# Router logits with the router's columns as weights, and 19 instead of 18 chunks of the shared network ahead of the expert tiles

## The chip, the cores and the metric

The kernel runs on one core of a Trainium2 chip. The metric is the device time of one execution in microseconds (us). TensorE does the matmuls, VectorE (DVE), ScalarE (ACT) and GpSimd (POOL) the elementwise work, SyncE (SP) starts most DMA transfers. Each engine executes its own list of instructions in program order and waits on semaphores that the other engines raise.

## The reference

```python
h = tok(x)                       # sin/cos of x at 6 frequencies, then a product with W: (4, 512, 192)
h = concat([cls_tok, h])         # 513 positions in each of 4 images
h = h + attn(layernorm(h))       # gated linear attention, elu features, running sums over positions
h = h + ffn(layernorm(h))

# ffn: 8 experts, 2 for each position, and a shared network of width 768
probs = softmax(x @ router_w)
gates, idx = top_k(probs, 2);  gates = gates / sum(gates)
routed = sum over the 2 experts of gate * ((silu(x @ w_gate[e]) * (x @ w_up[e])) @ w_down[e])
shared = silu(x @ ws_gate) * (x @ ws_up) @ ws_down
alpha  = sigmoid(x @ sg_w + sg_b)
return alpha * shared + (1 - alpha) * routed
```

## The kernel before

The positions go through in blocks: block 0 is the class token, blocks 1 to 4 are the four images of 512 positions. Every engine's list is written out by hand in one order.

The first two thirds are the token product. For every image `b` there are 9 groups `k`. POOL rounds (`rounds`, L406), DVE takes the remainder (`remainders`, L768 and L772), ACT takes the sines (`sines`, L477 and L480) and TensorE multiplies (`project(b, k)`, L1308: 24 matmuls, which show as 48 records because an fp32 matmul makes two passes). The features have 3 slots. Between the groups of image `b` each engine does one step of the attention of block `b` and of the router of block `b-1`: `attn1` (transposes of the normed input, L1319 and L1321), `attn2`, `attn2b`, `ranks`, `attn3` (L1364, which needs the keys that ACT's DMA moves, L533), `attn5` and so on to `attn8`. The router of a block is on TensorE `router(a)`, L1435 to L1439: for each of the 4 groups of 128 positions 5 fp32r matmuls, in which the positions are the 128 columns of weights and the 10 router columns stream. DVE's `router` copies the logits (L926), picks the top 2 and forms `dz`; ACT's `router` takes the exponential (L570); DVE's `gates`, `places` and POOL's `scatter` (L436) write every position's row into its expert's slots in DRAM.

After the last projection come the chunks of the shared network, `q` = 0 to 23, six for each image. `up(q)` is two products of 5 fp32r matmuls with 512 columns (L1463 to L1467), ACT takes the silu (L584), DVE multiplies (`hidden`, L1033), `down(q)` is 4 fp32 matmuls (L1501, 8 records). `finish(f)` on DVE (L1041) adds the six chunks of image `f` into H and frees the banks for `down` of the next image. `NQB` = 18 chunks stand ahead of the expert tiles; the attention and the router of block 4 lie between them at the places `Q_X1`, ..., `Q_LG` = 11 (router), `Q_RK` = 12 (ranks). SP then waits for all scatters and loads the slots (`xs`, L361). There are 39 tiles of 128 slots (`tile_x`, L1513 and L1514, `tile_up`, L1531 to L1535, `tile_hidden_t`, L1543, `tile_down`, L1553 and L1555); `down(NQB-2)` and `down(NQB-1)` stand inside the first two. Behind the tiles come the class token's shared network and the other 6 chunks, while the tiles' results return from DRAM (`yin`); DVE's `combine(b)` (L1109 and L1111) adds them, L1280 adds the last image's down product, and SP stores.

Of the kernel before, what the change touches and what calls it, by code (L numbers as in the profile page):

```python
# [16 lines left out]
B = 4  # L17
# [19 lines left out]
NQB = 18  # L37
# [26 lines left out]
XT, GU, HT, YB = (5, 6), (1, 0), 7, 2  # L64
# [17 lines left out]
def build(nc, xT, wT, freqs, cls_tok, packed, wsa, wsb, wds, wea, web, wdea, wdeb, blank, slots, ydram, out):  # L82
    with ExitStack() as ctx:
# [40 lines left out]
        wra_hi, wra_lo, wrb = (sb(n, [P, NR], F32R) for n in ("wra_hi", "wra_lo", "wrb"))  # L124
# [27 lines left out]
        with ExitStack() as fourth:  # L152
# [47 lines left out]
            lg_psum top_step dz_ready ez_ready gt_step oh_ready gates_ready rank_psum rk_ready pos_step slots_ready emap_ready  # L200
# [13 lines left out]
         lg_psum, top_step, dz_ready, ez_ready, gt_step, oh_ready, gates_ready, rank_psum, rk_ready, pos_step, slots_ready, emap_ready,  # L214
# [250 lines left out]
        def _(act):  # L465
# [181 lines left out]
            sines(0, 8)  # L647
            sines(1, 0)
# [3 lines left out]
            for b in range(1, B):  # L652
# [4 lines left out]
                if b >= 2:  # L657
                    router(b - 1)
                sines(b, 3)
# [20 lines left out]

            for q in range(NQB):
# [20 lines left out]
                if q == Q_LG:  # L702
                    router(B)
# [21 lines left out]
        def _(dve):  # L725
# [183 lines left out]
            def router(a):  # L909
# [12 lines left out]
                def wide(t):  # L922
# [3 lines left out]
                next_(dve.tensor_copy(lg[0:TP, 0:nt, :], ps[0:TP, logit_bank(a), 0:16 * nt].rearrange(  # L926
                    "p (t n) -> p t n", n=16)[:, :, 0:NE + 1]))
# [330 lines left out]
            finish(2)  # L1258
# [29 lines left out]
        def _(pe):  # L1288
            def project(a, k):
# [8 lines left out]
                for i in range(6):  # L1298
# [13 lines left out]
                ins.then_inc(tok_group, 1)  # L1312
# [113 lines left out]
            def router(a):  # L1426
# [344 lines left out]
```

## Time and profile before

| | |
|---|---|
| median of 3 runs | 581.56 us (580.43 to 583.87) |
| profiled execution | 580.34 us |
| its span | 578.5 us |
| TensorE busy | 557.0 us (96%) |
| DVE / ACT / POOL busy | 363.1 / 245.8 / 172.3 us |

The span is the time from the first to the last event of the profiled execution; 1.8 us of its time lie outside. The profile's stretches are: projections to about 368 us, chunks to 459, tiles from 462 to 546, the rest to 578.5.

### The profile page before, as it was taken

Reading aid. Unit: us, or ns where it says so; the run is one execution under the profiler, and the core shown is the slowest. Engines: PE = TensorE matmul, PEld = TensorE weight load, DVE = VectorE, ACT = ScalarE, POOL = GpSimd, SP = SyncE. Lnnn points to the kernel's source line nnn. Section 1 sums busy time; section 2 is a strip of 40 time slices with the busy share of each in tenths; the row PEclk is TensorE's granted clock in tenths of the full one; section 3 lists DMA queues with packets and bytes.
Section 4 is the critical chain, followed back from the end, with each engine's and each line's share of the span. In section 5 each row is a group of like instructions: output and inputs, shape, how many; then the busy total and the mean of one; then the engine's idle time right before and its main releaser. Section 6 shows DMA issues by size and latency. Waiting matters only on the chain.

```text
span 578.5 us, 9030 instructions
## 1 busy us (share of the span) xinstructions
PE 557.0 (96%) x3247; PEld 512.0 (88%) x3247; DVE 363.1 (63%) x1041; ACT 245.8 (42%) x342; POOL 172.3 (30%) x200
## 2 busy tenths in 40 slices
PE   2999999999999999999999999999999799999996
PEld 2998999798999989999979999977888699999775
DVE  5636787533768736779762796466877346666527
ACT  2455464755135653442565522253233135454310
POOL 5321332213215221674311460002201314444400
PEclk9998999999999999999999999999998999999999
DMA  8910048000000000210000010411100652431173
GB/s 296 331 37 19 1 155 289 29 0 28 13 25 20 19 0 10 74 55 1 1 0 10 20 46 10 141 78 38 47 1 19 197 183 82 133 95 55 50 219 109
DMA packets 23647, 42.48 MB, mean 73 GB/s; under 512 B 2662, under 2 KB 15204, under 8 KB 23508
## 3 DMA queue, kind: packets, MB, share of 16 engines
q1 hardware_dynamic: 19568, 33.31, 18.0%
q0 software_dynamic: 3472, 8.07, 3.9%
q10 hardware_dynamic: 564, 0.53, 0.4%
q8 instruction: 27, 0.44, 0.3%
q14 instruction: 16, 0.13, 0.1%
HBM read 31.73 MB, written 14.79 MB: 80 GB/s over the span
## 4 chain that ended last, share of the span: by engine, by line
PE 85%; DVE 6%; ACT 3%; DMA 3%; issue 2%; POOL 1%; ACTq 0%; DVEq 0%; POOLq 0%
PE ps L1308 46%; PE ps L1501 3%; PE ps L1387 2%; PE ps L1553 2%; PE ps L1555 2%; PE ps L1364 2%; PE ps L1463 1%; PE ps L1467 1%; PE ps L1465 1%; PE ps L1466 1%; PE ps L1464 1%; POOL slots L436 1%; PE ps L1531 1%; PE ps L1535 1%; PE ps L1532 1%
## 5 line engine op out<-in xcount | busy, mean ns | idle before, releaser
L1308 PE MATMUL ps<-w_tok,feat 128*128 128x192 f32 x1728 | 292.2, 330 | 11.6 <-ACT feat L472 10.3
L1308 PEld LDWEIGHTS ps<-w_tok,feat 128*128 128x128 f32 x1728 | 284.1, 192 | 15.0 <-issue 14.6
L406 POOL TENSOR_SCALAR feat<-x,f_col 128x512 int32<-128x512 f32 x108 | 91.5, 862 | 210.7 <-PE ps L1308 204.3
L477 ACT ACTIVATE feat<-feat 128x1536 f32<-128x1536 f32 x35 | 51.9, 1484 | 116.5 <-DVE feat L772 116.5
L768 DVE SCALAR_TENSOR_TENSOR feat<-x,f_col,feat 128x512 f32<-128x512 f32 x105 | 76.6, 783 | 1.4 <-POOL feat L406 0.9
L480 ACT ACTIVATE feat<-feat,half_pi 128x1536 f32<-128x1536 f32 x36 | 56.2, 1561 | 0.0
L442 POOL DMA_INDIRECT ydram<-yr,xs x39 | 37.4, 959 | 55.0 <-DVE yr L1082 55.0
L436 POOL DMA_INDIRECT slots<-pay_a,posi x17 | 18.4, 1083 | 74.2 <-DVE posi L1009 70.8
L1501 PE MATMUL ps<-w_down,hid_ring 128*128 128x192 f32 x192 | 37.6, 341 | 0.5 <-issue 0.4
L772 DVE TENSOR_SCALAR feat<-feat 128x1536 int32<-128x1536 int32 x35 | 37.2, 1062 | 1.2
L584 ACT ACTIVATE s_ring<-ps 128x512 f32<-128x512 f32 x24 | 14.4, 599 | 52.0 <-PE ps L1467 52.0
L1501 PEld LDWEIGHTS ps<-w_down,hid_ring 128*128 128x128 f32 x192 | 33.0, 197 | 2.8 <-issue 1.2
L1033 DVE TENSOR_TENSOR hid_ring<-s_ring,ps 128x512 f32<-128x512 f32 x24 | 16.4, 686 | 17.5 <-PE ps L1467 14.7
L1068 DVE TENSOR_TENSOR xlr<-ps,xhr 128x256 fp32r<-128x256 f32 x39 | 16.6, 425 | 16.3 <-ACT xhr L606 16.3
L606 ACT ACTIVATE xhr<-ps 128x256 fp32r<-128x256 f32 x39 | 15.0, 384 | 26.4 <-PE ps L1514 26.4
L1075 DVE TENSOR_TENSOR hidt<-sr,ps 128x192 f32<-128x192 f32 x39 | 13.8, 354 | 16.1 <-ACT sr L612 16.1
L1463 PE MATMUL ps<-X,wa_hi 128*128 128x512 f32 x48 | 22.5, 469 | 0.2 <-ACT s_ring L584 0.2
L814 DVE TENSOR_TENSOR_SCAN r<-one,s_c,r 128x512 f32<-128x512 f32 x4 | 5.1, 1284 | 27.4 <-ACT r L522 27.4
L1082 DVE TENSOR_SCALAR yr<-ps,xs 128x192 f32<-128x192 f32 x39 | 16.3, 418 | 8.6 <-PE ps L1555 8.6
L612 ACT ACTIVATE sr<-ps 128x192 f32<-128x192 f32 x39 | 12.9, 330 | 20.0 <-PE ps L1535 20.0
L1553 PE MATMUL ps<-wd_ea,htr 128*128 x78 | 19.2, 328 | 0.7 <-DVE yr L1082 0.7
L1465 PE MATMUL ps<-X,wa_hi 128*128 128x512 f32 x48 | 19.2, 401 | 0.0
(276 smaller groups left out, 857.0 us busy)
## 6 DMA issues: line engine op xcount, KB each, us to landing
slots<-in_blank SPq DMA_DIRECT2D x1, 5031.0 KB, 19.5
x<-in_xT SPq DMA_DIRECT2D x16, 256.0 KB, 2.6
w_tok<-in_wT SPq DMA_DIRECT2D x7, 576.0 KB, 10.2
xs<-slots SPq DMA_DIRECT2D x5, 645.0 KB, 5.8
yin<-ydram SPq DMA_DIRECT2D x8, 384.0 KB, 6.6
raw_a<-in_wea SPq DMA_DIRECT2D x4, 384.0 KB, 5.6
raw_b<-in_web SPq DMA_DIRECT2D x4, 384.0 KB, 6.3
w_tok<-in_wT SPq DMA_DIRECT2D x4, 288.0 KB, 8.5
```

Of the source, the lines that this page charges most:

```text
L406: ins = pool.tensor_scalar(feat[:, k % SLOTS, i, :].bitcast(I32), x[:, x_block(k), :], f_col[:, fi:fi + 1], 1.0, ALU.mult, ALU.mult)
L436: pool.indirect_dma_start(slots, bass.IndirectOffsetOnAxis(ap=idx, axis=0), (pay_a[a % 2], pay_b)[c][0:TP, t, :], None).then_inc(scat, 16)
L442: pool.indirect_dma_start(ydram, bass.IndirectOffsetOnAxis(ap=idx, axis=0), yr[:, s % NYR, :], None).then_inc(yscat[s % NYR], 16)
L477: act.activation(feat[:, k % SLOTS, 0:3, :], feat[:, k % SLOTS, 0:3, :], ACT.Sin, scale=TWO_PI).then_inc(sin_ready, 1)
L480: act.activation(feat[:, k % SLOTS, 3:6, :], feat[:, k % SLOTS, 3:6, :], ACT.Sin, bias=half_pi[:, :], scale=-TWO_PI).then_inc(sin_ready, 1)
L768: ins = dve.scalar_tensor_tensor(feat[:, s, i, :], x[:, x_block(k), :], f_col[:, fi:fi + 1], feat[:, s, i, :].bitcast(I32), ALU.mult, ALU. ...
L772: dve.tensor_scalar(feat[:, s, 3:6, :].bitcast(I32), feat[:, s, 0:3, :].bitcast(I32), 0x7FFFFFFF, None, ALU.bitwise_and).then_inc(r_ready, 1)
L1308: ins = pe.matmul(ps[:, TOK[a % 2][t // 2], (t % 2) * D:(t % 2 + 1) * D], feat[:, k % SLOTS, i, t * P:(t + 1) * P], w_tok[:, k, i, :], sta ...
L1463: pe.matmul(o, wa_hi[:, c, i, :], xh, start=True, stop=False)
L1465: pe.matmul(o, wa_hi[:, c, i, :], xl, start=False, stop=False)
L1501: ins = pe.matmul(ps[:, DN0 + t // 2, (t % 2) * D:(t % 2 + 1) * D], hid_ring[:, q % 3, t * P:(t + 1) * P], w_down[:, c, :], start=(c == 0 ...
L1553: pe.matmul(o, htr[:, s % 2, 0:P], wd_ea[:, bass.ds(e, 1), :].rearrange("p e n -> p (e n)"), start=True, stop=False)
```

## The change

The router is turned round. The router's columns are the weights, high and low part side by side in one tile `wra` of 20 columns, and 512 positions stream: 4 matmuls for a block. The result has 20 rows and 512 columns. ACT copies it to `lt` (`take_lt`), and TensorE transposes it back in 4 pieces (`router_rows`), which stand half a projection group later (after half of `project(0, 8)`, `project(2, 1)` and `project(3, 1)`, after `up(0)` for block 3 and after `down(9)` for block 4). DVE adds the high and the low half while it copies. In blocks 2 and 3 ACT's `router(b - 1)` moves behind `sines(b, 3)`.

The second part: NQB is 19, so chunk 18 (the first of the last image) stands ahead of the tiles, and the banks of the tiles are renamed to fit. `finish(2)` moves on DVE from behind the tiles to just behind the first `tile_low`. The two places of `combine` and `hidden` behind the tiles shift by one chunk.

```diff
-NQB = 18
+NQB = 19
-XT, GU, HT, YB = (5, 6), (1, 0), 7, 2
+XT, GU, HT, YB = (5, 6), (0, 2), 7, 1
...
+            def take_lt(a):
+                W, TP, nt = width(a)
+                act.wait_ge(lt_psum, a + 1)
+                act.activation(lt[:, 0:W], ps[0:2 * NR, logit_bank(a), 0:W], ACT.Copy).then_inc(lt_ready, 1)
...
                 attn1(b)
                 if b >= 2:
+                    take_lt(b - 1)
+                sines(b, 3)
+                if b >= 2:
                     router(b - 1)
-                sines(b, 3)
...
-                next_(dve.tensor_copy(lg[0:TP, 0:nt, :], ps[0:TP, logit_bank(a), 0:16 * nt].rearrange(
-                    "p (t n) -> p t n", n=16)[:, :, 0:NE + 1]))
+                halves = ps[0:TP, logit_bank(a), 0:32 * nt].rearrange("p (t c) -> p t c", c=32)[:, :, 0:2 * NR]
+                next_(dve.tensor_reduce(lg[0:TP, 0:nt, :], halves.rearrange("p t (h n) -> p t n h", h=2)[:, :, 0:NE + 1, :],
+                                        AX_X, ALU.add))
...
             for i in range(NTILE + 3):
                 if i < NTILE:
                     tile_low(i)
+                if i == 0:
+                    finish(2)
...
-            finish(2)
             hidden(NQB)
...
             hidden(NQB + 2)
             cls_shared()
+            combine(0)
             hidden(NQB + 3)
-            combine(0)
-            hidden(NQB + 4)
             combine(1)
             combine(2)
-            hidden(NQB + 5)
+            hidden(NQB + 4)
             combine(3)
...
-                for i in range(nt):
-                    o, c = ps[0:TP, logit_bank(a), 16 * i:16 * i + NR], slice(i * P, i * P + TP)
-                    pe.matmul(o, xh_a_[:, c], wra_hi[:, :], start=True, stop=False)
-                    pe.matmul(o, xh_a_[:, c], wra_lo[:, :], start=False, stop=False)
-                    pe.matmul(o, xl_a_[:, c], wra_hi[:, :], start=False, stop=False)
-                    pe.matmul(o, xh_b_[:, c], wrb[:, :], start=False, stop=False)
-                    ins = pe.matmul(o, xl_b_[:, c], wrb[:, :], start=False, stop=True)
+                if a >= 2:
+                    pe.wait_ge(rk_ready, a - 1)
+                o = ps[0:2 * NR, logit_bank(a), 0:W]
+                pe.matmul(o, wra[:, :], xh_a_, start=True, stop=False, skip_group_check=True)
+                pe.matmul(o, wra[:, :], xl_a_, start=False, stop=False, skip_group_check=True)
+                pe.matmul(o[0:NR], wrb[:, :], xh_b_, start=False, stop=False, skip_group_check=True)
+                pe.matmul(o[0:NR], wrb[:, :], xl_b_, start=False, stop=True, skip_group_check=True).then_inc(lt_psum, 1)
+
+            def router_rows(a):
+                W, TP, nt = width(a)
+                pe.wait_ge(lt_ready, a + 1)
                 for i in range(nt):
+                    ins = pe.transpose(ps[0:TP, logit_bank(a), 32 * i:32 * i + 2 * NR], lt[:, i * P:i * P + TP],
+                                       ident[0:2 * NR, 0:2 * NR])
                 ins.then_inc(lg_psum, 1)
```

TensorE in image 2, from the projections ahead of `attn1(2)` on, before (the five router rows stand four times, once for each group of positions; the last of these groups is shown):

```order
L1308 MATMUL ps<-w_tok,feat 128x192 x48
L1319 MATMUL ps<-pack,xn 128x128 x4
L1321 MATMUL ps<-pack,xn 64x128 x4
...
L1435 MATMUL ps<-wra_hi,X 128x10
L1436 MATMUL ps<-wra_lo,X 128x10
L1437 MATMUL ps<-wra_hi,X 128x10
L1438 MATMUL ps<-wrb,X 128x10
L1439 MATMUL ps<-wrb,X 128x10
L1308 MATMUL ps<-w_tok,feat 128x192 x24
L1345 MATMUL ps<-xt_a,pack 128x512
```

TensorE at the same place now (L1320 is the projection, L1458 `router_rows`):

```order
L1320 MATMUL ps<-w_tok,feat 128x192 x48
L1332 MATMUL ps<-pack,xn 128x128 x4
L1334 MATMUL ps<-pack,xn 64x128 x4
L1449 MATMUL ps<-X,wra 20x512
L1450 MATMUL ps<-X,wra 20x512
L1451 MATMUL ps<-X,wrb 10x512
L1452 MATMUL ps<-X,wrb 10x512
L1320 MATMUL ps<-w_tok,feat 128x192 x12
L1458 MATMUL ps<-pack,lt 128x20 x4
L1320 MATMUL ps<-w_tok,feat 128x192 x12
L1358 MATMUL ps<-xt_a,pack 128x512
```

Twenty matmuls have become four and four transposes, and the transposes stand behind half of the next projection group.

ACT in image 2, from the copy of `attn1` to the second copy of the values, before (L570 is the router's exponential, L514 and L517 are `odds`, L505 the values):

```order
L495 ACTIVATE xt_a<-ps 128x512
L570 ACT_TABLE_LOAD
L570 ACTIVATE ez<-dz 128x8
L477 ACT_TABLE_LOAD
L477 ACTIVATE feat<-feat 128x1536
L480 ACTIVATE feat<-feat,half_pi 128x1536
L514 ACT_TABLE_LOAD
L514 ACTIVATE r<-ps,pack 128x512
L517 ACTIVATE r<-r 128x512
L505 ACTIVATE v<-ps 128x2x192
```

The same stretch of ACT now (L571 is `take_lt`, L576 the router's exponential):

```order
L496 ACTIVATE xt_a<-ps 128x512
L571 ACTIVATE lt<-ps 20x512
L478 ACTIVATE feat<-feat 128x1536
L481 ACTIVATE feat<-feat,half_pi 128x1536
L576 ACT_TABLE_LOAD
L576 ACTIVATE ez<-dz 128x8
L515 ACTIVATE r<-ps,pack 128x512
L518 ACTIVATE r<-r 128x512
L506 ACTIVATE v<-ps 128x2x192
```

The exponential has moved behind the sines, one copy is new, and two table loads are gone.

DVE at the start of the tiles now (L1045 is `hidden`, L1080 `tile_low`, L1053 `finish(2)`, L1087 `tile_hidden`); before, three `hidden` stood in the first row shown and no row of `finish` among the others:

```order
L1045 TENSOR_TENSOR hid_ring<-s_ring,ps 128x512 x4
L1260 MEMSET hidt 128x2x64
L1080 TENSOR_TENSOR xlr<-ps,xhr 128x256
L1053 SCALAR_TENSOR_TENSOR H<-ps,alpha,H 128x192 x4
L1080 TENSOR_TENSOR xlr<-ps,xhr 128x256
L1087 TENSOR_TENSOR hidt<-sr,ps 128x192
```

The four instructions of `finish(2)` now stand between the first two `tile_low`.

## Rows read from the trace of the kernel before

**Rows 1.** The page, part 1: busy time, share of the span, instructions.

```profile
PE 557.0 (96%) x3247; PEld 512.0 (88%) x3247; DVE 363.1 (63%) x1041; ACT 245.8 (42%) x342; POOL 172.3 (30%) x200
```

**Rows 2.** Windows of 1 us, TensorE: busy, granted clock, DMA share, GB/s.

```profile
436.00:437.00 1.00, 1.00 (x4) 0.50 0.00 0
...
463.00:464.00 1.00, 1.00 (x3) 0.50 1.06 334
```

**Rows 3.** Timeline of TensorE in image 2: start, us, what.

```profile
191.08 0.25 PE L1435 MATMUL ps<-wra_hi,X 128*128 128x10 f32 x1
...
193.31 8.05 PE L1308 MATMUL ps<-w_tok,feat 128*128 128x192 f32 x48
...
224.32 2.42 PE L1364 MATMUL ps<-r 64*128 64x512 f32 x8
```

**Rows 4.** The chain that ended last: a 512-column matmul, four transposes.

```profile
431.24 0.23 PE ps L1465
...
376.11 0.44 PE ps L1321 x4
```

**Rows 5.** Timeline of DVE in image 2.

```profile
193.49 0.20 DVE L926 COPY lg<-ps 128x36 f32<-128x36 f32 x1 [0.61 <-PE ps L1439]
...
207.22 2.07 DVE L768 SCALAR_TENSOR_TENSOR feat<-x,f_col,feat 128x512 f32<-128x512 f32 x3
```

**Rows 6.** L772 over the span: ns min, median, max.

```profile
L772 DVE TENSOR_SCALAR feat<-feat x35: 959/960/1344, 16.2 to 348.6; 128x1536 int32<-128x1536 int32 x35
```

**Rows 7.** Timeline of ACT in image 2.

```profile
195.05 0.58 ACT L495 ACTIVATE xt_a<-ps 128x512 f32<-128x512 f32 x1
...
210.31 1.48 ACT L477 ACTIVATE feat<-feat 128x1536 f32<-128x1536 f32 x1 [1.82 <-DVE feat L772]
...
216.20 0.49 ACT L505 ACTIVATE v<-ps 128x384 f32<-128x384 f32 x1 [2.94 <-PE ps L1336]
...
222.08 0.47 ACTq L533 DMA_DIRECT2D r<-r  x1
```

**Rows 8.** DMA of L533, issue to landing.

```profile
DMA to landing us min/median/max: 1.7/2.2/2.2
```

**Rows 9.** Timeline of TensorE at Q_LG: the router of block 4 and what follows.

```profile
431.77 0.17 PE L1435 MATMUL ps<-wra_hi,X 128*128 128x10 f32 x1
...
433.92 1.98 PE L1501 MATMUL ps<-w_down,hid_ring 128*128 128x192 f32 x8
```

**Rows 10.** Timeline of DVE from Q_LG to the tiles.

```profile
434.53 0.20 DVE L926 COPY lg<-ps 128x36 f32<-128x36 f32 x1
...
444.87 1.39 DVE L1041 SCALAR_TENSOR_TENSOR H<-ps,alpha,H 128x192 f32<-128x192 f32 x4
```

**Rows 11.** The chain that ended last, at the load of the slots.

```profile
459.79 2.12 DMA xs<-slots
```

**Rows 12.** Timeline of TensorE from the last chunk to the tiles.

```profile
446.76 1.46 PE L1501 MATMUL ps<-w_down,hid_ring 128*128 128x192 f32 x8
...
457.64 1.46 PE L1501 MATMUL ps<-w_down,hid_ring 128*128 128x192 f32 x8
462.05 0.32 PE L1513 MATMUL ps<-pack,xs 128*128 128x128 f32 x1 [2.95 <-DMA xs<-slots]
...
462.95 2.86 PE L1501 MATMUL ps<-w_down,hid_ring 128*128 128x192 f32 x8 [0.36 <-issue]
...
469.12 0.27 PE L1543 MATMUL ps<-pack,hidt 128*128 128x128 f32 x1
```

**Rows 13.** Timeline of DVE behind the tiles.

```profile
563.09 0.69 DVE L1033 TENSOR_TENSOR hid_ring<-s_ring,ps 128x512 f32<-128x512 f32 x1 [2.18 <-PE ps L1467]
...
566.66 0.69 DVE L1033 TENSOR_TENSOR hid_ring<-s_ring,ps 128x512 f32<-128x512 f32 x1 [1.02 <-PE ps L1467]
...
574.23 1.37 DVE L1280 SCALAR_TENSOR_TENSOR H<-ps,alpha,H 128x192 f32<-128x192 f32 x4
```

**Rows 14.** Window of 1 us behind the tiles, as in Rows 2.

```profile
560.00:561.00 1.00, 1.00 (x6) 1.00 0.30 100
```

More of the change, by code:

```diff
@@ L123, in build @@
         wr_raw = part("wr").rearrange("p (h n) -> p h n", h=2)
-        wra_hi, wra_lo, wrb = (sb(n, [P, NR], F32R) for n in ("wra_hi", "wra_lo", "wrb"))
+        wra, wrb = sb("wra", [P, 2 * NR], F32R), sb("wrb", [P, NR], F32R)
+        lt = sb("lt", [2 * NR, T])
         f_col = sb("f_col", [P, NF + 3])
@@ L199, in build @@
             xpose2 nta_ready ntb_ready wo_psum h2_ready xn2_ready xpose3 xh_ready xl_ready
-            lg_psum top_step dz_ready ez_ready gt_step oh_ready gates_ready rank_psum rk_ready pos_step slots_ready emap_ready
+            lt_psum lt_ready lg_psum top_step dz_ready ez_ready gt_step oh_ready gates_ready rank_psum rk_ready pos_step slots_ready emap_ready
             payb_ready scat
@@ L213, in build @@
          xpose2, nta_ready, ntb_ready, wo_psum, h2_ready, xn2_ready, xpose3, xh_ready, xl_ready,
-         lg_psum, top_step, dz_ready, ez_ready, gt_step, oh_ready, gates_ready, rank_psum, rk_ready, pos_step, slots_ready, emap_ready,
+         lt_psum, lt_ready, lg_psum, top_step, dz_ready, ez_ready, gt_step, oh_ready, gates_ready, rank_psum, rk_ready, pos_step, slots_ready, emap_ready,
          payb_ready, scat,
@@ L647, in _ @@
             sines(0, 8)
+            take_lt(0)
             sines(1, 0)
@@ L678, in _ @@
                 take_h(b)
+            take_lt(B - 1)
             for q in range(NQB):
@@ L702, in _ @@
                 if q == Q_LG:
+                    take_lt(B)
                     router(B)
@@ L1145, in _ @@
             attn1(0)
-            dve.tensor_copy(wra_hi[:, :], wr_raw[:, 0, :])
+            dve.tensor_copy(wra[:, 0:NR], wr_raw[:, 0, :])
             dve.tensor_copy(wrb[:, :], wr_raw[:, 1, :]).then_inc(router_split, 1)
             dve.wait_ge(router_split, 1)
-            dve.tensor_tensor(wra_lo[:, :], wr_raw[:, 0, :], wra_hi[:, :].bitcast(F32), ALU.subtract)
+            dve.tensor_tensor(wra[:, NR:2 * NR], wr_raw[:, 0, :], wra[:, 0:NR].bitcast(F32), ALU.subtract)
             dve.tensor_tensor(wrb[DB:P, :], wr_raw[DB:P, 1, :], wrb[DB:P, :].bitcast(F32),
@@ L1288, in _, with project @@
         def _(pe):
-            def project(a, k):
+            def project(a, k, recs=range(6)):
                 q = NG * a + k
@@ L1297, in project @@
                     pe.wait_ge(h_ready, a - 1)
-                for i in range(6):
+                for i in recs:
                     if q == 0 and i < 2:
@@ L1311, in project @@
                                         skip_group_check=True)
-                ins.then_inc(tok_group, 1)
+                if 5 in recs:
+                    ins.then_inc(tok_group, 1)
             def attn1(a):
@@ L1608, in _ @@
             router(0)
-            project(0, 8)
+            project(0, 8, range(3))
+            router_rows(0)
+            project(0, 8, range(3, 6))
             for b in range(1, B):
@@ L1616, in _ @@
                     router(b - 1)
-                project(b, 1)
+                project(b, 1, range(3))
+                if b >= 2:
+                    router_rows(b - 1)
+                project(b, 1, range(3, 6))
                 attn2(b)
@@ L1638, in _ @@
                 up(q)
+                if q == 0:
+                    router_rows(B - 1)
                 if q == Q_X1:
@@ L1661, in _ @@
                     down(q - 2)
+                if q == Q_LG:
+                    router_rows(B)
             pe.wait_ge(emap_ready, 1)
```

## The prediction

> **What bounds the kernel now.** The page's first part comes first: TensorE is busy for 557.0 us, 96% of the span [rows 1]. DVE at 63% and ACT at 42% bind only where TensorE waits for them. So the question is where TensorE idles, where it runs slowly, and what it does too much of. The timeline of TensorE shows the largest wait behind the start: it ends its last chunk's `down(15)` at about 458.9 (start 457.64 and 8 records, 1.3 us) and waits 2.95 us for the slots, until 462.05 [rows 12]. The chain of waits has the transfer of the slots there, which follows POOL's scatters and, before them, the router of block 4 [rows 11]. The windows show the granted clock: 0.50 of full (1.2 instead of 2.4 GHz) right after this wait, and once more after the router of block 4 [rows 2]. What that costs is in the durations: 8 records of `down` show 2.86 us after the wait and 1.46 elsewhere, 1.98 after the router, where the fall begins in their midst [rows 9, 12]. Last comes the end: DVE and not TensorE starts the last additions, at 574.23 [rows 13].
>
> **The router's own cost.** In image 2 the 20 matmuls take from 191.08 to 193.31, 2.23 us [rows 3]. A 512-column fp32r matmul follows the next by 0.23 us, four transposes take 0.44 us [rows 4]. The new router is 4 x 0.23 + 0.44 = 1.36 us, 0.87 less. (The transposes stream only 20 columns but load 128 columns of weights as those of the row do; I take the row.) Five blocks: block 0 has 2 columns and is worth nothing; blocks 1 to 3 are 3 x 0.87 = 2.6 us; block 4 is treated below. If nothing else moved, that would be the gain of the first part.
>
> **What the later logits do in images 2 and 3.** Now DVE waits longer. It gets its logits at 193.49 before [rows 5]. After: the four matmuls end at 192.0, half a projection group is 3.95 us (48 records in 8.05 with the last one's drain, 7.9 without [rows 3]), so 195.95. ACT ends `xt_a` at 195.63 and needs about 0.5 more for `lt` [rows 7], so 196.15: TensorE waits 0.2 there. The transposes and their latency give 196.8, 3.3 us later than before; the reduce is 0.05 longer than the copy (an estimate, twice the elements). DVE's `remainders(2, 3)` queue behind, then ACT's sines, then (new order) ACT's exponential with its table load, then `odds`; `gates`, which waits for the exponential, holds `negatives`. So `remainders(2, 4)`, at 207.22 before [rows 5], come 3.3 us later, and so do `sines(2, 4)`, at 210.31 before [rows 7]. In addition `remainders(2, 3)` now fall on POOL's rounding: where both run, L772 takes 1.34 instead of 0.96 [rows 6], 0.4 more. Sum 3.7 us. The cover: ACT waited 2.94 us for TensorE before it took the second values, at 216.20 [rows 7]. So 0.75 us remain, and they stand on a chain without slack: values, logarithm, running sum, powers, the key DMA issued at 222.08, 2.2 us to landing, that is 224.28, and TensorE's `attn3` at 224.32 [rows 3, 7, 8]. Hence `attn3` starts 0.75 later than before, not 0.65 earlier, and TensorE idles about 1.4 us there. Image 3 has the same order of work. Cost 2 x 0.75 = **+1.5 us**, in place of a gain of 1.7. Bounds: the whole 3.7 passes, +7.4; or nothing does, -1.7.
>
> For POOL and DVE at one SBUF port the Trainium skill (SBUF — State Buffer, "Who interferes with whom") says that the second to issue blocks fully until the first is done. By it the overlap could cost up to one rounding more. The 1.34 of L772 is the measured case and is used here.
>
> **Block 3 and block 0.** Router 3 stands in front of `up(0)`, its transposes behind `up(0)`, while ACT's copy is long done. Of its 0.87 I take **-0.5**: the transposes of block 4's `attn1` soon wait for DVE's layer norm, which does not move (bounds 0 and -0.9). Block 0's later logits delay DVE ahead of image 1's layer norm by about a microsecond, most of it idle time of DVE; 0 (bounds 0 and +0.5).
>
> **From Q_LG to the tiles.** Before, the router of block 4 takes 431.77 to 433.92 [rows 9] and DVE copies at 434.53 [rows 10]. Now: 0.93 for the matmuls, then `down(9)`, 1.3, then transposes: the logits are there at 434.65, +0.2 with the longer reduce. DVE, ACT and POOL then go as before, so the slots land at 459.79 + 2.12 + 0.2 = 462.1 [rows 11]. TensorE itself saves 0.8, and its fall of clock, 1.5 us, may vanish, since no stretch with 10 columns per load is left. Neither helps: `down(12)` must wait for `finish(1)`, at 444.87 for 1.39 us [rows 10], so it starts at 446.5 and not before, where it had 446.76 [rows 12]. From there on TensorE is 0.26 ahead. `down(15)` ends at 458.7, chunk 18 adds ten matmuls, 2.33 [rows 4], and `down(16)` 1.3: 462.3. The slots are there by then. No wait, and no fall of clock.
>
> **The tiles' start.** From 462.3: two transposes and register loads 0.5, `down(17)` 1.3 at full clock (2.86 before), to 464.15. `finish(2)` needs it and takes 1.39 on DVE, to 465.7 [rows 10]. Meanwhile TensorE has two transposes and `tile_up(0)`, about 1.1, and stands before `down(18)` with about 0.5 to wait. Then `down(18)` 1.3, transposes 0.2, `tile_up(1)` 0.9: the first transposes of the hidden rows start at 468.1, before at 469.12 [rows 12]. **-1.0 us**. Bounds: +0.7, when the clock falls all the same (1.7 more), and -1.5, without the wait for `finish(2)`.
>
> **The end.** From there to the last tile nothing changes. Behind the tiles TensorE does one chunk less, 2.33 + 1.3 = 3.63. Does DVE follow? The third of its last four `hidden`, at 563.09, had 2.18 us of idle time before it [rows 13], and `combine(0)`, 1.93 us, now stands in that gap; its data has landed, the DMA share falls in the window at 560 [rows 14]. Then everything follows as it did from 566.66 [rows 13], 563.09 in its place: 3.57 earlier. **-3.6 us**; bounds -2.5 (if `combine(0)` must wait for data) and -3.7.
>
> **The sum.** +1.5 - 0.5 - 1.0 - 3.6 = **-3.6 us** against the profiled 580.34, which gives 576.7. The median shown is 581.56, 1.2 above that execution; against it I get **578.0**.
>
> **Clock, page and row.** The row shows 0.50 after 2.95 us of idle time [rows 2, 12]. The Trainium skill (TensorE: Matmul & The Clock Gate, "Part 1: The HAM clock gate") says that the default is the throttled state, activity releases it, and idle gaps between bursts bring it back; here the trace agrees. The sum goes by the rows: it counts one fall fewer at the tiles.
>
> **Rivals.** (B) *The delay hides.* DVE's or ACT's lateness is taken up (for instance because two table loads on ACT are gone), `attn3` starts as early as TensorE gets there: 2 x (-0.65 - 0.75) = -2.8 more, 575.2. For it: the margin of 0.75 is a small difference of long terms. Against: the DMA's slack of 0.04. (C) *The clock falls in a new wait.* The new waits (1.4 us at `attn3`, twice, and up to 1.3 before `down(12)`) are shorter than the 2.95 that preceded a fall, but the stretch of the router, 2.15 us with no idle time at all, preceded one too. One fall costs about 1.5: 579.5; three cost 4.5: 582.5. That section of the page speaks for this one. (D) *The chunk is no gain at the front:* the slots are not the limit, the PE reaches the tiles late and waits for `finish(2)` in full, the tiles start 1.5 later than before instead of 1.0 earlier: 580.5. It would be the case that the second part merely moves work. (E) *Slower:* the late sines. If ACT's 2.94 us of cover are not there for the moved work (ACT does the exponential between the sines and `odds`, `gates` waits for it, and all of DVE stands behind), all 3.7 pass to `attn3` in both images: +5.9 more than in the sum, 583.9. The point from which it decides: the sum has 3.6 us to lose, 1.8 in each image, so the cover would have to be under 1.1 us instead of 2.94.
>
> **Chances.** Forecast 0.45, B 0.19, C 0.18, D 0.11, E 0.07. The measurement of this kernel tells about 0.5% from no change, 2.9 us, which puts the bound at 578.65. The forecast is close to it, so a fifth of its chance falls to "same"; B is faster; C and D are the same except for a piece (three falls, 0.02 slower). Faster 0.36 + 0.19 = 0.55, slower 0.07 + 0.02 = 0.09, same the rest, 0.36. Range 575.0 to 581.0: it takes in B, one fall of clock and D. The forecast's own range is 577.0 to 579.0.
>
> **What would show it.** In the changed profile: TensorE waiting for the key DMA at L1377 (`attn3`) for over a microsecond in images 2 and 3, nothing of it in B; ACT's second values without an idle gap before them; no idle time over 0.5 us before the first `tile_x`, and full clock there; a wait of about 0.5 us before `down(18)`, with `finish(2)` as its releaser; a wait before `down(12)` for `finish(1)`; the tiles' first transpose of hidden rows about 1 us earlier relative to the router of block 4; and from the last tile to the end 3.6 us less. The prediction is wrong if the clock falls at other places than now, if the transposes with 20 rows cost more than 0.11 us each, or if the tile loop itself gets another pitch through its renamed banks.

## The result, and the profile after

The changed kernel takes 577.87 us (median of 6 runs, 575.85 to 579.51), the kernel before 581.77 in the same runs. The ratio is 0.9915, with a 95% interval of 0.9888 to 0.9941: faster by 0.85%, which is 4.9 us (3.4 to 6.5). The two medians as they stand differ by less, 3.90 us, which lies inside that interval. 578.0 had been predicted. The profiled execution took 577.9, with a span of 576.1, that is 2.4 less than the span of before, where the prediction had summed 3.6. So the time fits better than the steps do, and the steps are what is examined here.

The page of after, part 1, in the columns of [rows 1]:

```profile
PE 554.3 (96%) x3199; PEld 505.4 (88%) x3199; DVE 363.2 (63%) x1041; ACT 242.1 (42%) x343; POOL 176.4 (31%) x200
```

TensorE is busy for 2.7 us less. Now its waits, each a sum over the span, with number and longest. The wait of 2.95 us for the slots [rows 12] is gone from the list, and three others stand in it:

```profile
PE ps L1377 <- DMA r<-r: 1.9, 3, 0.9
PE ps L1521 <- DVE H L1053: 1.6, 2, 1.1
PE ps L1470 <- DVE oh L952: 0.5, 1, 0.5
```

L1377 is `attn3`, waiting for the key DMA: 0.82 us in image 2, 0.85 in image 3, and 0.18 in image 1, which before has as well (0.19). L1521 is `down`, waiting for `finish`. L1470 is `ranks`. The timeline of TensorE in image 2, which answers to [rows 3]:

```profile
191.26 0.47 PE L1449 MATMUL ps<-X,wra 128*20 128x512 f32 x1
...
192.26 4.06 PE L1320 MATMUL ps<-w_tok,feat 128*128 128x192 f32 x24
196.34 0.42 PE L1458 MATMUL ps<-pack,lt 20*128 20x20 f32 x4
196.69 3.52 PE L1320 MATMUL ps<-w_tok,feat 128*128 128x192 f32 x20
...
224.72 2.42 PE L1377 MATMUL ps<-r 64*128 64x512 f32 x8 [0.82 <-DMA r<-r]
```

The router is 192.26 - 191.26 = 1.00 us, its transposes 196.69 - 196.34 = 0.35, together 1.35 in place of 2.23. None of it arrives: from the router to `attn3` are 33.46 us, before 33.24. DVE and ACT of the same image, in the columns of [rows 5, 7] (L938 is the reduce of the logits, L783 the remainders, L971 the start of `gates`):

```profile
196.80 0.23 DVE L938 TENSOR_REDUCE lg<-ps 128x36 f32<-128x72 f32 x1 [3.73 <-PE ps L1458]
...
201.95 1.25 DVE L783 TENSOR_SCALAR feat<-feat 128x1536 int32<-128x1536 int32 x1
207.74 0.17 DVE L971 TENSOR_SCALAR iz<-ez 128x8 f32<-128x8 f32 x1 [4.54 <-ACT ez L576]
```

```profile
213.76 1.48 ACT L478 ACTIVATE feat<-feat 128x1536 f32<-128x1536 f32 x1 [2.07 <-DVE feat L783]
215.15 1.56 ACT L481 ACTIVATE feat<-feat,half_pi 128x1536 f32<-128x1536 f32 x1
216.62 0.47 ACT L506 ACTIVATE v<-ps 128x384 f32<-128x384 f32 x1
...
222.48 0.47 ACTq L534 DMA_DIRECT2D r<-r  x1
```

The logits come 3.3 us later than before, `sines(2, 4)` 3.45 later, and ACT no longer has idle time before the second values, where it had 2.94 [rows 7]. What is over passes to the key DMA (222.48, before 222.08) and to `attn3`.

How the lateness gets from the logits to the next remainders shows in two waits of DVE. Before, `negatives` (L801) waited 4.70 us for TensorE:

```profile
205.22 0.69 DVE L801 TENSOR_SCALAR r<-ps 128x512 f32<-128x512 f32 x1 [4.70 <-PE ps L1348]
```

After, that wait is gone, and `gates` (L971) waits 4.54 us for ACT's exponential, which now stands behind the sines. The chain that ended last, in after, goes through it (L576 is the table load and then the exponential):

```profile
206.20 1.28 ACT L576
207.50 0.22 ACT ez L576
207.74 0.18 DVE iz L971
```

Then the clock, in the windows of [rows 2]:

```profile
226.00:227.00 1.00, 1.00 (x6) 0.75 (x4) 0.86 (x7) 0.00 (x0) 0.00 (x0) 1.00 0.00 0
227.00:228.00 1.00, 1.00 (x5) 0.94 (x4) 0.93 (x4) 0.00 (x0) 0.00 (x0) 0.56 0.00 0
228.00:229.00 1.00, 1.00 (x5) 1.00 (x4) 1.00 (x3) 0.00 (x0) 0.00 (x0) 0.50 0.00 0
```

The third value from the end is the granted clock: it falls at 227.1, 2.4 us behind the restart at 224.72, with TensorE busy all the time since, and is back at 230.6. From `attn3` of image 2 to the router of the next block are 61.44 us, before 59.83: 1.6 lost. Behind the same wait in image 3 the clock stays at 1.00. The tiles (compare [rows 12]), then the end on DVE (compare [rows 13]):

```profile
464.20 0.27 PE L1533 MATMUL ps<-pack,xs 128*128 128x128 f32 x1
...
464.76 1.56 PE L1521 MATMUL ps<-w_down,hid_ring 128*128 128x192 f32 x8 [0.18 <-issue]
...
467.90 1.54 PE L1521 MATMUL ps<-w_down,hid_ring 128*128 128x192 f32 x8 [0.49 <-DVE H L1053]
...
470.38 0.27 PE L1563 MATMUL ps<-pack,hidt 128*128 128x128 f32 x1
```

```profile
561.71 0.41 DVE L1108 SCALAR_TENSOR_TENSOR h_c<-ps,alpha,h_c 2x192 f32<-2x192 f32 x1 [2.66 <-PE ps L1605]
562.15 0.96 DVE L1121 TENSOR_TENSOR H<-H,yin 128x768 f32<-128x768 f32 x1
563.14 0.96 DVE L1123 TENSOR_TENSOR H<-H,yin 128x768 f32<-128x768 f32 x1
564.23 0.69 DVE L1045 TENSOR_TENSOR hid_ring<-s_ring,ps 128x512 f32<-128x512 f32 x1
...
571.79 1.37 DVE L1292 SCALAR_TENSOR_TENSOR H<-ps,alpha,H 128x192 f32<-128x192 f32 x4
```

The first `tile_x` has no wait before it and `down(17)` runs at full speed. `combine(0)` (562.15 and 563.14) stands in the gap ahead of `hidden(22)`, and the last additions start at 571.79 instead of 574.23.

### The profile page after: what moved, and what is told of

Same layout as the page of the kernel before. It is cut to its first block, busy times and chain, and to the rows that moved or that the text cites. A ratio compares the mean times of both kernels' runs of the same rounds, so it can differ in the third digit from the quotient of the medians.

```text
span 576.1 us, 8938 instructions
## 1 busy us (share of the span) xinstructions
PE 554.3 (96%) x3199; PEld 505.4 (88%) x3199; DVE 363.2 (63%) x1041; ACT 242.1 (42%) x343; POOL 176.4 (31%) x200
## 3 DMA queue, kind: packets, MB, share of 16 engines
q0 software_dynamic: 3472, 8.07, 3.9%
## 4 chain that ended last, share of the span: by engine, by line
PE 76%; DVE 13%; ACT 7%; DMA 2%; issue 2%; ACTq 0%; POOL 0%; DVEq 0%
PE ps L1320 39%; PE ps L1521 4%; PE ps L1400 2%; PE ps L1573 2%; PE ps L1575 2%; DVE feat L779 2%; PE ps L1377 2%; ACT feat L478 2%; PE ps L1483 1%; PE ps L1551 1%; PE ps L1486 1%; PE ps L1484 1%; PE ps L1487 1%; PE ps L1485 1%; PE ps L1555 1%
## 5 line engine op out<-in xcount | busy, mean ns | idle before, releaser
L1320 PE MATMUL ps<-w_tok,feat 128*128 128x192 f32 x1728 | 295.0, 332 | 11.0 <-ACT feat L473 9.7
L1320 PEld LDWEIGHTS ps<-w_tok,feat 128*128 128x128 f32 x1728 | 286.4, 193 | 14.9 <-issue 14.0
L407 POOL TENSOR_SCALAR feat<-x,f_col 128x512 int32<-128x512 f32 x108 | 95.2, 896 | 209.2 <-PE ps L1320 202.9
L783 DVE TENSOR_SCALAR feat<-feat 128x1536 int32<-128x1536 int32 x35 | 38.1, 1089 | 1.2
L1521 PE MATMUL ps<-w_down,hid_ring 128*128 128x192 f32 x192 | 35.9, 330 | 1.9 <-DVE H L1053 1.6
L1521 PEld LDWEIGHTS ps<-w_down,hid_ring 128*128 128x128 f32 x192 | 31.6, 189 | 4.9 <-issue 3.1
L1045 DVE TENSOR_TENSOR hid_ring<-s_ring,ps 128x512 f32<-128x512 f32 x24 | 16.4, 685 | 17.9 <-PE ps L1487 15.0
L1087 DVE TENSOR_TENSOR hidt<-sr,ps 128x192 f32<-128x192 f32 x39 | 13.8, 354 | 15.7 <-ACT sr L618 15.3
L1080 DVE TENSOR_TENSOR xlr<-ps,xhr 128x256 fp32r<-128x256 f32 x39 | 16.5, 424 | 10.6 <-ACT xhr L612 10.6
L1483 PE MATMUL ps<-X,wa_hi 128*128 128x512 f32 x48 | 22.0, 457 | 0.2 <-ACT s_ring L590 0.2
L437 POOL DMA_INDIRECT slots<-pay_b,posi x17 | 18.0, 1061 | 5.2 <-issue 5.2
L1575 PE MATMUL ps<-wd_eb,htr 128*128 x78 | 19.1, 326 | 0.0
```

Of the source, the lines that this page charges most:

```text
L407: ins = pool.tensor_scalar(feat[:, k % SLOTS, i, :].bitcast(I32), x[:, x_block(k), :], f_col[:, fi:fi + 1], 1.0, ALU.mult, ALU.mult)
L437: pool.indirect_dma_start(slots, bass.IndirectOffsetOnAxis(ap=idx, axis=0), (pay_a[a % 2], pay_b)[c][0:TP, t, :], None).then_inc(scat, 16)
L783: dve.tensor_scalar(feat[:, s, 3:6, :].bitcast(I32), feat[:, s, 0:3, :].bitcast(I32), 0x7FFFFFFF, None, ALU.bitwise_and).then_inc(r_ready, 1)
L1320: ins = pe.matmul(ps[:, TOK[a % 2][t // 2], (t % 2) * D:(t % 2 + 1) * D], feat[:, k % SLOTS, i, t * P:(t + 1) * P], w_tok[:, k, i, :], sta ...
L1483: pe.matmul(o, wa_hi[:, c, i, :], xh, start=True, stop=False)
L1521: ins = pe.matmul(ps[:, DN0 + t // 2, (t % 2) * D:(t % 2 + 1) * D], hid_ring[:, q % 3, t * P:(t + 1) * P], w_down[:, c, :], start=(c == 0 ...
```

## The experiments

A span carries the accidents of one execution: router 1 starts anywhere from 188.1 to 191.5 us in the twelve traces, partly with a fall of the clock at about 49 us, in the first image, that some executions have and others don't. So the traces are compared by stretches, each the difference of two starts on TensorE's timeline (the last one ends with the start of DVE's last additions). r2 to r4 are the routers of the next blocks, "th" the first transposes of hidden rows, "last" the second half of the last tile's `tile_down`.

| kernel | router 1 to attn3(2) | to r2 | to attn3(3) | r3 to r4 | r4 to th | th to last | to the end |
|---|---|---|---|---|---|---|---|
| before | 33.24 | 59.83 | 33.22 | 63.28 | 37.35 | 76.27 | 28.84 |
| after | 33.46 | 61.44 | 33.44 | 63.03 | 36.70 | 76.23 | 25.18 |
| e1 | 33.48 | 61.44 | 33.47 | 63.06 | 38.19 | 76.18 | 28.80 |
| e2 | 33.25 | 59.82 | 33.23 | 63.28 | 36.76 | 76.25 | 25.22 |
| e3 | 32.74 | 59.77 | 32.55 | 63.06 | 37.28 | 76.15 | 25.19 |
| e4 | 32.77 | 59.77 | 32.57 | 63.34 | 37.76 | 76.21 | 28.82 |
| e5 | 32.78 | 59.77 | 32.56 | 62.80 | 37.11 | 76.15 | 25.19 |
| e6 | 32.76 | 59.77 | 32.56 | 63.34 | 40.55 | 76.16 | 24.36 |
| e7 | 33.46 | 61.45 | 33.44 | 63.03 | 37.15 | 76.19 | 27.12 |
| e8 | 38.88 | 64.69 | 38.87 | 63.34 | 36.80 | 76.16 | 25.19 |
| e9 | 32.86 | 59.77 | 33.45 | 63.06 | 37.18 | 76.23 | 25.18 |
| e10 | 33.47 | 61.45 | 32.55 | 63.04 | 37.23 | 76.19 | 25.20 |

Two columns carry a scatter of their own. From r4 to "th" the code of after, e3, e7, e8, e9 and e10 is the same, and the stretch is 36.70 to 37.28. The difference arises at the first tile: the first `tile_x` starts 30.52 us behind r4 in after and 30.66 to 30.77 in e3, e7, e9 and e10, and ahead of `down(17)` TensorE then has 0.18 us of idle time in after and 0.47 or 0.48 in those four. From r3 to r4 the ten kernels with the new router have 63.03 to 63.06, but e4, e6 and e8 63.34 and e5 62.80. In these two columns a difference of half a microsecond between two traces shows nothing.

**e1 and e2: one part of the change each.** e1 keeps the new router and undoes the rest:

```diff
-NQB = 19
+NQB = 18
-XT, GU, HT, YB = (5, 6), (0, 2), 7, 1
+XT, GU, HT, YB = (5, 6), (1, 0), 7, 2
```

with `finish(2)` behind the tiles and `combine(0)` in its old place. e2 has the same lines the other way round, in the kernel before.

> The change's router with everything of the chunk part as before (18 chunks ahead of the tiles, the old banks, finish(2) behind the tiles, combine(0) in its old place). Theory (the two parts add up, and the new router gives its TensorE work away again): attn3 of images 2 and 3 each start about 0.2 us later counted from their router, block 3 gives back 0.45, and from block 4's router to the tiles the slots decide, 0.2 later than before. That is about +0.4 us against the profiled execution of before (580.34): 580.7, and 1.6 more, 582.3, where the clock falls behind the wait at attn3 of image 2, as it did in the profiled execution of after. TensorE waits about 3.3 us for the slots, and the clock is 0.50 behind it as before; after block 4's router it stays 1.00. Rival (the router's saving of 0.87 us in four blocks reaches the end): 576.9, with no wait over 0.5 us at attn3.

> The change's 19 chunks, banks, finish(2) among the tiles and combine(0) ahead of the next hidden, with the old router (20 matmuls with 10 columns). Theory: nothing moves before the tiles and the clock still falls at about 435; down(16) ends at about 462.5, behind the landing of the slots, so there is no wait of microseconds before the first tile_x and no fall of the clock there; the first transposes of hidden rows start 0.3 us earlier than before (468.8), and the last additions start 4.0 earlier (570.2). Sum -4.0: 576.3 against the 580.34 of before's profiled execution, that is less than the change as a whole has where its clock falls. Rival (the chunk only moves work, the gain of the whole change is the router's): at most 0.5 us from before.

e1: 582.55 us (582.3 expected with the fall, which its trace has), ratio 0.9999 (0.9976 to 1.0022). e2: 576.41, ratio 0.9894 (0.9861 to 0.9926). The forecast of e2 was 576.3. The router alone gains nothing, the chunk alone has the whole gain. The rivals of both fall. e1 at the tiles:

```profile
464.33 0.30 PE L1533 MATMUL ps<-pack,xs 128*128 128x128 f32 x1 [3.69 <-DMA xs<-slots]
...
465.23 2.26 PE L1521 MATMUL ps<-w_down,hid_ring 128*128 128x192 f32 x8 [0.49 <-issue]
```

TensorE waits 3.69 us there instead of 2.95 [rows 12], and the clock falls behind it as in before. e2 has the first `tile_x` without a wait. It also has no fall of the clock after the router of block 4, although that router is the old one and all ahead of it is as before: that goes against its expectation, and so the fall at 434.9 [rows 2] is no property of that code alone. It also makes e2's time a partly lucky hit, since its forecast had counted this fall.

**e3 and e4: remainders ahead of the router on DVE.** e3 is the changed kernel with this edit, e4 is e1 with it:

```diff
-                if b >= 2:
-                    router(b - 1)
                 remainders(b, 3)
+                if b >= 2:
+                    router(b - 1)
                 if b >= 2:
                     gates(b - 1)
```

> The changed kernel with one order changed on DVE: remainders(b, 3) stand ahead of router(b-1) instead of behind it. DVE waited 3.73 us for the logits in image 2, and POOL's rounding of that group had ended, so they fit (2.07 + about 1 us) into the wait. Theory (attn3's wait is the late sines passed on): ACT's sines(2, 4) start at about 210.3 again instead of 213.8, ACT waits for TensorE again before the second values, attn3 of images 2 and 3 start 0.65 us and more earlier than in before, counted from their router, without a wait over 0.2 us for the key DMA, and with that wait the fall of the clock behind attn3 of image 2 is gone. Against after without the fall (574.5 of span) two times 0.87 less: span 572.8, time 574.6. Rival 1 (the key DMA's chain runs with fixed latencies from TensorE's own values, the sines don't set it): attn3 moves by 0.65 with a wait as before's, 0.2 each. Rival 2 (the clock falls by the work around it and not by this wait): the fall at about 225 stays, 576.2.

> The new router without the chunk part (18 chunks, as in e1), and DVE's remainders(b, 3) ahead of router(b-1), as in e3. Theory: it differs from e1 by the same 1.7 us as e3 does from after, and by the fall of the clock where e1 has it: 579.0, 1.4 under before's profiled execution, of which images 2 and 3 give 1.3 and block 3 0.45, with 0.2 lost again in the slots. TensorE waits over 3 us for the slots. Rival (TensorE's savings ahead of the tiles are all swallowed by the wait for the slots, since these come by a chain of DVE, POOL and DMA that is not shortened): 580.4 as before.

e3: 574.73 us, ratio 0.9864 (0.9840 to 0.9889), forecast 574.6. e4: 579.49, ratio 0.9954 (0.9929 to 0.9979), forecast 579.0. DVE of e3 in image 2:

```profile
190.49 2.08 DVE L779 SCALAR_TENSOR_TENSOR feat<-x,f_col,feat 128x512 f32<-128x512 f32 x3 [0.54 <-POOL feat L407]
192.60 0.96 DVE L783 TENSOR_SCALAR feat<-feat 128x1536 int32<-128x1536 int32 x1
193.69 0.23 DVE L938 TENSOR_REDUCE lg<-ps 128x36 f32<-128x72 f32 x1
```

The remainders fill the 3.73 us that DVE waited for the logits, and the reduce follows without idle time. The same image on ACT, and then on TensorE:

```profile
206.71 1.49 ACT L478 ACTIVATE feat<-feat 128x1536 f32<-128x1536 f32 x1 [1.82 <-DVE feat L783]
...
212.59 0.49 ACT L506 ACTIVATE v<-ps 128x384 f32<-128x384 f32 x1 [2.93 <-PE ps L1349]
```

```profile
220.87 2.42 PE L1377 MATMUL ps<-r 64*128 64x512 f32 x8
```

ACT waits 2.93 us again ahead of the second values, as it did in [rows 7], and `attn3` doesn't wait. The stretches to it are 0.72 and 0.89 shorter than in after, and the 1.6 of the fall are gone. So the late sines were the cause of the wait (rival 1 falls), and in this trace there is no fall without the wait (rival 2 falls).

**e5: two waits for `finish` shortened.** On DVE `finish(1)` moves ahead of `hidden(13)`, on TensorE `down(NQB - 1)` moves from `i == 1` to `i == 2`:

```diff
-                if i == 1:
+                if i == 2:
                     down(NQB - 1)
```

> The kernel of e3 with two waits for finish shortened: finish(1) stands ahead of hidden(13) instead of ahead of hidden(14), and down(18) one tile later, behind tile_up(1), where finish(2) is long done. Theory: down(12) waits 0.5 instead of 1.10 us, down(18) not at all instead of 0.49. In e3 the slots were issued at 455.79 and take 2.2 us to land, TensorE reached the first tile_x at 458.13, so they have 0.1 us to spare: the first saving turns into a wait of about 0.5 us for the slots, only the second counts. -0.6 against e3: 574.1. Rival 1 (the slots are not at their limit): both count, -1.1. Rival 2 (the clock falls behind the wait for the slots even at half a microsecond): +1.1 against e3.

574.79 us, ratio 0.9859 (0.9814 to 0.9904), the same as e3; 574.1 had been expected. From r4 to "th" it has 37.11 us, e3 37.28: 0.2 instead of 0.6, and 0.2 lies inside the scatter of that column. TensorE of e5:

```profile
460.26 0.30 PE L1535 MATMUL ps<-pack,xs 128*128 128x128 f32 x1 [0.26 <-DMA xs<-slots]
...
464.71 0.44 PE L1553 MATMUL ps<-e_hi,xhr 128*128 x1 [0.70 <-DVE xlr L1080]
```

The first saving turned into a wait for the slots, as expected (0.26 us, 0.5 expected); the second into one that I had not seen, `tile_up(1)` waiting 0.70 us for DVE's split of the tile, for which `down(18)` had been the cover.

**e6: 20 chunks.** The kernel of e3 with these lines, and with the moves on DVE and TensorE that the expectation names:

```diff
-NQB = 19
+NQB = 20
-XT, GU, HT, YB = (5, 6), (0, 2), 7, 1
+XT, GU, HT, YB = (5, 6), (2, 1), 7, 0
```

> The kernel of e3 with 20 chunks ahead of the tiles (banks renamed accordingly, finish(2) ahead of the tiles, down(18) and down(19) in the second and third tile, combine(0) and combine(1) ahead of hidden(23), combine(2) and combine(3) behind it). Theory (the 19th chunk paid by the wait for the slots, and none is left to fill): the tiles start 3.6 us later less about 0.5 for down(18)'s wait, TensorE does 3.63 less behind them, but DVE has one gap of 2.9 us less for its four combines of 1.9 us each: 2 to 3 us of the saving don't arrive. 574.7 + 2.5 = 577.2. Rival (every chunk that moves ahead gains, since the end is bound by its chunks): 571.1.

577.65 us, ratio 0.9902 (0.9863 to 0.9940); forecast 577.2. The interval of its ratio just overlaps that of e3 (0.9840 to 0.9889), so the stretches have to decide. The tiles come 3.3 us later than in e3 (40.55 against 37.28), and only 0.8 is given back at the end (24.36 against 25.19). The last `down` says why: it waits for DVE, which has four combines in the last two gaps:

```profile
567.73 1.57 PE L1519 MATMUL ps<-w_down,hid_ring 128*128 128x192 f32 x8 [1.13 <-DVE hid_ring L1045]
```

**e7: `combine(0)` back.** The changed kernel with

```diff
-            combine(0)
             hidden(NQB + 3)
+            combine(0)
             combine(1)
```

> The changed kernel with combine(0) behind the next hidden instead of ahead of it, the order that it had before against its neighbours. Theory (the gap that DVE had ahead of hidden(22), 2.66 us at L1108, carries combine(0), and the three combines behind hidden(22) would take 5.7 us where TensorE needs 3.6): from the last tile's yr to the start of the last additions 26.4 us instead of 24.65, time 579.6. Rival (TensorE's chunks alone set the end): unchanged, 577.9.

The stretch to the end grew by 1.94 us (27.12 against 25.18; 1.75 expected), and the last `down` waits for DVE:

```profile
568.91 2.47 PE L1521 MATMUL ps<-w_down,hid_ring 128*128 128x192 f32 x8 [2.10 <-DVE hid_ring L1045]
```

The time, 577.7 us where 579.6 was expected, doesn't show it. The ratio, 0.9933 (0.9902 to 0.9964) against 0.9915, leans that way, and the intervals overlap. Between two such kernels the stretch decides: it is 25.18 to 25.22 us in the seven traces that have 19 chunks and `combine(0)` in the gap, and 27.12 in e7. The gap on DVE carries `combine(0)`.

**e8: the delay doubled.** The changed kernel with the transposes behind the whole group in images 2 and 3:

```diff
-                project(b, 1, range(3))
+                project(b, 1)
                 if b >= 2:
                     router_rows(b - 1)
-                project(b, 1, range(3, 6))
```

> The changed kernel with the transposes of the logits behind the whole group project(b, 1) instead of in its middle, in images 2 and 3: the logits come 3.95 us later still. Theory (the cover of 2.94 us on ACT is used up in after, all further lateness of the sines reaches attn3): TensorE waits for the key DMA at attn3 for about 4.7 us in image 2 and in image 3 instead of 0.82 and 0.85; +7.8 in all, and each of these waits has a fall of the clock behind it, one more than after: 577.9 + 7.8 + 1.7 = 587.4. Rival (the 0.82 comes from the DMA queue and not from the late sines): the waits stay near 0.8, 578.5.

595.36 us, ratio 1.0202 (1.0146 to 1.0259); 587.4 had been expected. The mechanism is the one expected, the size was missed by 8 us. TensorE in image 2:

```profile
229.70 4.63 PE L1377 MATMUL ps<-r 64*128 64x512 f32 x8 [6.33 <-DMA r<-r]
234.27 10.77 PE L1320 MATMUL ps<-w_tok,feat 128*128 128x192 f32 x48
```

The wait is 6.33 us, not 4.7 (6.36 in image 3), and `attn3` shows 4.63 in place of 2.42, the next group 10.77 in place of 8.07. The first rows below, of DVE, show where the longer wait comes from; the windows behind them show the clock:

```profile
200.66 0.62 DVE L943 TENSOR_TENSOR key<-lg,top 128x32 f32<-128x32 f32 x1
201.32 0.63 DVE L944 TENSOR_TENSOR key<-key,pack 128x32 f32<-128x32 f32 x1
201.99 0.19 DVE L945 TENSOR_REDUCE top<-key 128x4 f32<-128x32 f32 x1
...
214.64 2.77 DVE L779 SCALAR_TENSOR_TENSOR feat<-x,f_col,feat 128x512 f32<-128x512 f32 x3
```

```profile
226.00:227.00 1.00, 0.00 (x0) 0.00 (x0) 0.32 (x1) 0.65 (x1) 0.44 (x1) 0.57 0.00 0
...
239.00:240.00 1.00, 1.00 (x6) 1.00 (x4) 0.97 (x2) 0.00 (x0) 0.69 (x2) 0.60 0.07 25
```

Where DVE's chain lies beside POOL's rounding (199.88 to 201.91 and 213.75 to 216.21 on POOL's timeline), single steps take 0.62 instead of 0.19 and the remainders 2.77 instead of 2.07, 1.6 us together. And here the clock falls during the wait, at 226.1, and is low until 239.8: 13.7 us in place of the 3.4 in after. In image 3, where after has no fall, it falls during the wait too, at 332.0, and is low until 342.2. The stretches give the account of the missing 8 us: the two up to `attn3` are 5.4 longer than in after, where 3.9 was expected, and the two behind it, each from `attn3` to the next router, 3.3 and 4.3, where 1.7 was expected for one more fall.

**e9 and e10: which wait has the fall.** The edit of e3 in image 2 alone, and in image 3 alone.

> The order of e3 (remainders(b, 3) ahead of router(b-1) on DVE) in image 2 alone; image 3 keeps the order of the changed kernel and its wait of 0.85 us at attn3. So far the granted clock fell behind attn3 of image 2 in all three traces that have a wait of 0.8 us there (after, e1, e7) and in none of those without it (before, e2 to e6), and never behind the same wait in image 3. Theory (it is the wait at that place that the fall needs): no fall between 200 and 560 us; 574.73 of e3 plus 0.85: 575.6. Rival (a wait of 0.8 us brings one fall wherever it comes first, and image 3 was spared because image 2 had had its fall): a fall behind attn3 of image 3, 577.3.

> The order of e3 in image 3 alone; image 2 keeps the order of the changed kernel and its wait of 0.82 us at attn3. Theory: the clock falls behind attn3 of image 2 as in after, e1 and e7, and not in image 3; 574.73 plus 0.8 for the wait and 1.7 for the fall: 577.2, so that the fall alone is the difference from the kernel with the order in image 2 alone. Rival (the falls in image 2 came by chance with the wait): no fall there, 575.6.

e9: 575.66 us, ratio 0.9890 (0.9856 to 0.9924). e10: 575.82, ratio 0.9892 (0.9854 to 0.9929). e9's time is the 575.6 of its theory. e10's is not: its theory said 577.2, its rival 575.6. The traces did what the theory said: e9 has 0.85 us of wait in image 3 and no fall from 200 to 560 us, e10 has the fall behind image 2:

```profile
222.66 2.42 PE L1379 MATMUL ps<-r 64*128 64x512 f32 x8 [0.83 <-DMA r<-r]
225.01 9.75 PE L1322 MATMUL ps<-w_tok,feat 128*128 128x192 f32 x48
```

The medians don't separate the two, and neither does the mean granted clock of the six runs of each (0.9955 in e9, 0.9952 in e10), so a cost of the fall in the time of these kernels isn't shown. The stretches behind `attn3(2)` do separate them, 61.45 us against 59.77, in one trace each. In eleven traces (all but e8's) the clock fell behind `attn3` of image 2 in all four that wait 0.82 or 0.83 us there (after, e1, e7, e10) and in none of the seven that wait 0.22 or less. Behind the wait of 0.84 to 0.87 in image 3 it fell in none of four (after, e1, e7, e9).

## Why the prediction was right, and where it was not

**The router's own cost: right.** 1.36 us predicted, 1.35 measured. Two small errors cancel in it: the four matmuls take 1.00, not 0.92, and the transposes 0.35, not 0.44.

**Images 2 and 3: right that the gain turns into a loss, wrong in the size.** "So 0.75 us remain" was the step: it put `sines(2, 4)` 3.7 us later, and they came 3.45 later, of which 0.18 had been there at the router. Counted from the router, the logits were 3.1 late instead of 3.3, and the overlap with POOL cost 0.29 (L783 1.25, before 0.96), not 0.4. 3.27 less the cover of 2.94 leaves 0.33; 0.24 of it reached the second values and 0.22 `attn3` in each image: +0.4 in both, where I had +1.5. Over a microsecond of wait at `attn3` was named as the sign of the forecast, and it is 0.82 and 0.85. e3 shows the cause by taking it away, e8 by more of it.

One link of that step held by luck. It passed the 3.3 us of the logits straight on to `remainders(2, 4)`. But before, DVE waited 4.70 us for TensorE ahead of `negatives`, which the prediction doesn't mention and which is longer than the 3.3. The lateness came through because `gates` now waits 4.54 us for the exponential, which was moved behind the sines; the slack that was lost and the wait that was added are nearly equal. So part of the wait at `attn3` may belong to that move on ACT and not to the late logits. No run keeps ACT's old order with the new router, and this rival stays untested.

**Rival C came true, once.** The prediction let the clock fall nowhere new. It fell behind `attn3` of image 2, 1.6 us, after a wait that I had judged too short beside 2.95. With it these images cost +2.0 instead of +1.5, for other reasons than stated. By the prediction's own last condition (the clock falls at other places than now) its account is wrong in this point, although its time fits. The Trainium skill (TensorE: Matmul & The Clock Gate, "Part 1: The HAM clock gate") says that idle gaps between bursts bring the throttled state back. The three waits of 2.95 to 3.69 us for the slots (before, e1, e4) and the 0.82 in image 2 agree with it; the 0.84 to 0.87 in image 3, four times without a fall, shows that the length of one wait alone doesn't decide. What does is open.

**Block 3: too large in size, its sign not firm.** From r3 to r4 0.25 less, with 0.45 gained by `attn3` of block 4 and 0.2 lost at a wait for its layer norm. -0.5 was taken. In seven of the ten traces with the new router the stretch is 0.22 to 0.48 shorter than in before and e2 (63.28), in three it is 0.06 longer: e4 and e6 wait 0.42 and 0.45 us there for ACT's silu.

**From Q_LG to the tiles: right in its waits, too large in size.** 36.70 us from the router to "th", before 37.35: 0.65 less, where -1.0 was taken. The waits stand where they were named: `down(12)` for `finish(1)`, 1.09 us, `down(18)` for `finish(2)`, 0.49, none at the first `tile_x`. Up to the first `tile_x` the sum is exact (30.52 us behind the router, 30.53 predicted). Behind it `down(17)` and `down(18)` take 1.4 each rather than the 1.3 of my sum, and the two handovers around `finish(2)` are 0.14 longer. The wait of 0.49 at `ranks` costs nothing here, since `down(12)` waits for DVE behind it and starts where it was predicted. And 0.65 is the best of six: in the four traces of e3, e7, e9 and e10, with the same code in this stretch, only 0.07 to 0.20 is saved, in e8 0.55.

**The end: right.** 28.84 - 25.18 = 3.66 us, 3.6 predicted; e7 shows that the gap on DVE carries it.

**The sum.** +0.4 for the images, +1.6 for the clock, -0.25, -0.65 and -3.66 give -2.6, and with the 0.18 by which router 1 starts later that is the -2.4 of the span. The runs say -4.9 (3.4 to 6.5), the medians -3.9. Much of the gap is in before: its profiled execution, 580.34 us, lies 1.4 under its median of 581.77, while that of after, 577.90, lies at its median. The profiled execution of before had a mean granted clock of 0.991. Beside the experiments before was run 52 times: 37 runs have 0.986 or less and a median of 582.8 us, 15 have more and a median of 580.8, while after has 0.993 or 0.997 in all six. So most executions of before lose more to the clock than the one profiled. Where they lose it, no trace shows, and that this is all of the difference is argued.

So the total was hit by luck as much as by the steps. Between the profiled executions -3.6 was predicted and -2.4 measured, 1.2 too much, above all for the fall of the clock that I left out in after. The prediction then carried the 1.2 between before's profiled execution and its median over to after, where there is no such difference. The two errors have the same size and cancel: 578.0 against 577.87.

**The best of these kernels** are e3 and, level with it, e5: 574.73 us for e3, 1.36% under before, against 0.85% for the change. The chunk part alone (e2, 0.9894) is as good as the whole change. The router part is worth something only with DVE's order mended: 0.9954 in e4 against 0.9999 in e1.

## What to carry to other kernels

When a result is made later on purpose, look at what stands behind its consumer in the same queue, and put the work that is ready ahead of the wait; that edit was worth more here (e4 against e1, 3.1 us between the medians) than the faster operation, which alone was worth nothing (e1 against before). Work moved into a wait pays only as far as the wait is long (19 chunks yes, 20 no, e2 and e6), and a wait that is shortened shows the next one right behind it (e5). Where accidents of the start and the clock are as large as the effect, compare stretches between landmarks, and trust the span of neither execution.

## What the runs showed of the hardware

The granted clock fell at the same place in 4 of 4 traces with a wait of 0.8 us, and in 0 of 4 at another place with nearly the same wait; with the same code ahead of it, it fell after the router of block 4 in before and not in e2. After 6.3 us of idle time in e8 it came back only 10.1 us after TensorE had started again (229.70 to 239.8), and 8.9 in image 3; after 0.82 us in after it was low for 3.4 us.

Small DVE operations with 32 elements a row took 0.62 us instead of 0.19 beside POOL's rounding (e8, in both images). POOL's three instructions of that group take 2.03 us from 199.88, a third each if they are equal, so the second ends at about 201.23 and the third at 201.91; DVE's L943 ends at 201.28 and L944 at 201.95. The reduce before them (200.44, 0.19 us, one input), beside the first two, was not held up. The Trainium skill (SBUF — State Buffer, "Who interferes with whom") says that a DVE instruction with two inputs in SBUF contends with GpSimd's reads, that the one that comes second blocks until the other is done, and that a reduce doesn't contend; these rows agree, with one instruction of POOL as the unit.

The 24 fp32 matmuls of a projection group show as 48 records, the 4 of a `down` as 8. What the two records of such a matmul are inside, no run of this case shows.
